# A four-layer mixture-of-experts block: rope's turning in four transfers, the gather a step ahead, combine first, exp behind the copies

## The reference

```python
# x: 16 sequences of 256 rows and 128 columns
h = layernorm(x) * (1 + ca) + sa
x = x + ga * wavelet_attention(h)           # the prologue
h = layernorm(x) * (1 + cb) + sb
for l in range(4):                          # the loop of this study
    h = rms(x, ln1_w[l])
    q, k, v = h @ wq[l], h @ wk[l], h @ wv[l]     # 16 query heads, 4 key heads of 64
    q, k = q * cos + rot_half(q) * sin, k * cos + rot_half(k) * sin
    a = softmax(q k^T / 8 + causal) v
    x = clip(x + a @ wo[l], -100, 100)
    h = rms(x, ln2_w[l])
    # 8 experts of width 256, the two best of each row, weighted by their softmax
    x = clip(x + sum_e comb_e * (silu(h @ wg[l, e]) * (h @ wu[l, e])) @ wd[l, e], -100, 100)
x = x1 + gb * x
```

## Time and profile before

| | |
|---|---|
| median of 3 runs | 3637.83 us (3637.82 to 3639.13) |
| profiled execution | 3605.28 us, span 3603.5 us |
| mean granted clock of PE | 0.891 |
| busy share PE, DVE, ACT, Pool | 75%, 63%, 56%, 52% |

### The profile page before, as it was taken

How to read it: one execution, slowest core, us unless ns; L and a number is a source line. 1 busy time by engine, 2 the same in 40 slices (tenths; PEclk the granted TensorE clock), 3 DMA queues, 4 the chain that set the end, 5 groups by cost and what they waited for, 6 DMA issues and landing times.

```text
span 3603.5 us, 67188 instructions
## 1 busy us (share of the span) xinstructions
PE 2710.9 (75%) x20406; PEld 2157.3 (60%) x20406; DVE 2263.4 (63%) x8164; ACT 2015.8 (56%) x7080; POOL 1860.3 (52%) x1662
## 2 busy tenths in 40 slices
PE   5227777788778887888778876888778877887573
PEld 2225555666657665676567765676566665676462
DVE  5775555666666666666666665675666766666343
ACT  3126556566656656666556665665666665666321
POOL 0025555545565556555665556545665565555413
PEclk9558888999999999999989998999999998999765
DMA  9112222555236642555255633654256622553374
GB/s 377 70 49 62 62 64 62 163 179 172 69 116 200 214 126 85 165 179 155 65 162 183 211 100 95 190 166 137 67 180 208 195 84 90 178 180 111 124 253 132
DMA packets 327990, 511.67 MB, mean 142 GB/s; under 512 B 56353, under 2 KB 175681, under 8 KB 327105
## 3 DMA queue, kind: packets, MB, share of 16 engines
q1 hardware_dynamic: 311248, 473.79, 42.5%
q0 software_dynamic: 16384, 33.59, 3.0%
HBM read 316.58 MB, written 106.69 MB: 117 GB/s over the span
## 4 chain that ended last, share of the span: by engine, by line
PE 37%; ACT 16%; DVE 15%; POOL 14%; SPq 7%; DMA 6%; issue 5%; POOLq 0%; DVEq 0%
ACT arena L1049 9%; PE psum L778 6%; SPq L626 5%; PE psum L796 5%; POOL rows_in L1274 5%; POOL arena L1283 4%; DVE arena L1546 3%; DMA arena<-arena 3%; PE psum L846 2%; PE psum L753 2%; DVE arena L1568 2%; PE psum L798 2%; PE psum L896 2%; DMA arena<-rows_out,arena 2%; POOL arena L1300 2%
## 5 line engine op out<-in xcount | busy, mean ns | idle before, releaser
L1049 ACT ACTIVATE arena<-arena 128x128 f32<-128x128 f32 (+1 forms) x2048 | 900.9, 446 | 46.8 <-DVE arena L1572 46.8
L1283 POOL TENSOR_TENSOR arena<-arena 128x512 f32<-128x512 f32 (+1 forms) x512 | 743.9, 1476 | 251.4 <-DVE arena L1577 249.2
L778 PE MATMUL psum<-arena 128*128 128x128 f32 x3072 | 509.8, 308 | 384.3 <-ACT arena L1056 192.4
L1300 POOL TENSOR_TENSOR arena<-arena 128x512 f32<-128x512 f32 x320 | 409.5, 1280 | 573.5 <-DMA arena<-arena 573.2
L778 PEld LDWEIGHTS psum<-arena 128*128 128x128 f32 x3072 | 368.1, 154 | 506.0 <-ACT arena L1056 258.0
L1056 ACT COPY arena<-psum 128x384 f32<-128x384 f32 x1024 | 450.9, 480 | 284.0 <-PE psum L778 283.0
L1581 DVE COPY arena<-psum 128x512 f32<-128x512 f32 x256 | 176.4, 689 | 553.9 <-PE psum L798 553.9
L753 PE MATMUL psum<-arena 64*128 64x128 f32 (+1 forms) x4096 | 445.3, 358 | 10.9 <-DVE arena L1568 6.0
L1568 DVE CUSTOM_DVE_ANT_0 arena<-psum,arena 128x256 f32<-128x256 f32 x1024 | 429.6, 420 | 0.0
L1546 DVE TENSOR_TENSOR arena<-psum,arena 128x512 f32<-128x512 f32 x640 | 390.5, 675 | 7.4 <-POOL arena L1300 4.1
L1049 ACT ACTIVATION_READ_ACCUMULATOR arena<-arena 128x1 f32 x2048 | 389.7, 190 | 0.0
(11 more groups left out here) (199 smaller groups left out, 5608.4 us busy)
## 6 DMA issues: line engine op xcount, KB each, us to landing
gu<-gu_kept SPq DMA_DIRECT2D x320, 512.0 KB, 4.4
arena<-arena SPq DMA_DIRECT2D x1280, 64.0 KB, 2.0
wd<-wd_kept SPq DMA_DIRECT2D x320, 256.0 KB, 4.1
arena<-rows_in SPq DMA_DIRECT2D x320, 64.0 KB
rows_out<-arena SPq DMA_DIRECT2D x320, 64.0 KB, 2.6
rows_in<-arena SPq DMA_DIRECT2D x34, 512.0 KB, 7.5
rows_out<-arena SPq DMA_DIRECT2D x34, 512.0 KB, 7.0
gu_kept<-w_hi SPq DMA_DIRECT2D x32, 256.0 KB
```

Of the source, the lines that this page charges most:

```text
L778: mm = T.transpose(psum[:, t_bank(key), j * P:(j + 1) * P], probs[:, q, i, j * P:(j + 1) * P], ident)
L1049: ins = A.activation(a, a, ACT.Exp, bias=negmax[:, q, k:k + 1], accum_out=rowsum[:, q, k:k + 1])
L1283: ins = G.tensor_tensor(a, a, r[:, :, t:t + 1].broadcast_to([P, 4, P * (t + 1)]), ALU.mult)
L1300: G.tensor_tensor(QKT[it % 2][:, 2 * u:2 * u + 2, :].rearrange("p a b -> p (a b)"), own_part[:, k, :], turned_part[:, k, :], ALU.add).then ...
```

## The change

- Rope: the columns of wq and wk and the tables are reordered so that the two halves of a head lie on alternate partitions (`halves_in_turn`). A swap of neighbours then takes two transfers for a group of units: 3 units, then 2, so four a step for twenty. `to_turn` and `turned_part` hold all five units; the cosine product goes straight to QKT, and Pool adds in place after one wait a group.
- Pool: root stands ahead of normalise(0) and of the gather, scatter(it - 2) stands behind root (it was scatter(it - 1) at the step's end), and the gather is for it + 2, behind normalise(0), or behind normalise(2) at the end of a batch.
- DVE: combine stands ahead of place 0.
- ACT: square_rows and scale_rows come earlier; exp(0) stands behind copies(2), exp(1) behind copies(3) and ahead of the copy of v; exp(2) and exp(3) are cut in two around the first part of places 5 and 7; copy_y comes after the second part.
- One half-step of each batch is moved from place 7 of step 6 to place 6 of step 5.

```diff
+def halves_in_turn(w):
+    lead = w.shape[:-1]
+    return np.swapaxes(w.reshape(*lead, w.shape[-1] // HD, 2, HD // 2), -2, -1).reshape(w.shape)
...
-                          (5, (0, 1, 2, 3, 4, 5, 7)), (6, (0, 1, 2, 3, 4, 5, 7))):
+                          (5, range(8)), (6, range(6))):
...
 # turn_halves, SP
-                for u in units:
-                    n = 5 * it + u
-                    k = n % ROPE_RING
-                    s_was_read(sp, ("qk", it, u))
-                    for r in range(4):
-                        here, there = r * 32, (r ^ 1) * 32
-                        sp.dma_start(turned_part[there:there + 32, k, :], to_turn[here:here + 32, k, :]) \
-                            .then_inc(sem(f"turned_in{k}"), 16)
+                s_was_read(sp, ("qk", it, units[-1]))
+                us = slice(units[0], units[-1] + 1)
+                for r in range(2):
+                    sp.dma_start(turned_part[1 - r:P:2, us, :], to_turn[r:P:2, us, :]) \
+                        .then_inc(sem(f"turned_in{units[0]}"), 16)
...
 # ACT, the loop
+            def moe_end(b, hs):
+                if hs % 2 == 1 and hs > 1:
+                    copy_y(b * PT + hs // 2 - 1)
...
                 place(it, 0)
+                place_end(it, 0)
                 if old:
                     copy_probs(it - 1, 2)
-                place(it, 1)
-                if now:
-                    exps(it, 0)
-                if old:
-                    copy_probs(it - 1, 3)
-                if now:
-                    copy_v(it)
-                place(it, 2)
-                if now:
-                    exps(it, 1)
                 if coming:
                     square_rows(it + 1)
-                place(it, 3)
+                if now:
+                    exps(it, 0)
+                place(it, 1)
+                place_end(it, 1)
+                if old:
+                    copy_probs(it - 1, 3)
+                if now:
+                    exps(it, 1)
+                    copy_v(it)
                 if coming:
                     scale_rows(it + 1)
+                place(it, 2)
+                place_end(it, 2)
+                place(it, 3)
+                place_end(it, 3)
...
+                if now:
+                    exps(it, 2, range(2))
                 place(it, 5)
                 if now:
-                    exps(it, 2)
+                    exps(it, 2, range(2, 4))
+                place_end(it, 5)
...
 # Pool, the loop
-                if coming and it + 1 >= B:
-                    gather(it + 1)
-                if now:
-                    normalise(it, 0)
                 if coming:
                     root(it + 1)
+                if it >= 2:
+                    scatter(it - 2)
+                if now:
+                    normalise(it, 0)
+                if B <= it + 2 < NIT and (it + 2) % HB != 0:
+                    gather(it + 2)
...
                 if now:
                     normalise(it, 2)
+                if B <= it + 2 < NIT and (it + 2) % HB == 0:
+                    gather(it + 2)
                 if coming:
                     rope_adds(it + 1, range(N_QK1, N_QK))
-                if old:
-                    scatter(it - 1)
...
 # DVE, the loop
                 if old:
                     invert(it - 1, 3)
+                if coming and it + 1 >= B:
+                    combine(it + 1)
                 place(it, 0)
...
-                if coming and it + 1 >= B:
-                    combine(it + 1)
                 if old:
                     update_x(it - 1)
```

More of the change, by code:

```diff
@@ L342, in bass_program @@
         tiles = arena.take(2).bitcast(U32)
-        ROPE_RING = 3
         dead_at_end = arena.at
-        own_part = arena.take(ROPE_RING, 512)
-        to_turn = arena.take(ROPE_RING, 512)
-        turned_part = arena.take(ROPE_RING, 512)
+        to_turn = arena.take(N_QK, 512)
+        turned_part = arena.take(N_QK, 512)
         QKT = [arena.take(2 + NH // 2, S) for _ in range(2)]
@@ L384, in bass_program @@
         back_last = arena.take(LAST_RING, ST, 2, C)
[L385 removed]
+        assert arena.at <= dead_at_end + 2 * N_QK * 512 + 2 * (2 + NH // 2) * S
         ZERO_ROWS = 8
@@ L453, in gate_side, with keys_and_queries @@
             return U_AT["gate", g, j] % U_RING
+        def keys_and_queries(it, u):
+            return QKT[it % 2][:, 2 * u:2 * u + 2, :].rearrange("p a b -> p (a b)")
         def kv_head(q, half):
@@ L618, in turn_halves @@
             def turn_halves(it, units):
-                for u in units:
-                    n = 5 * it + u
-                    k = n % ROPE_RING
-                    s_was_read(sp, ("qk", it, u))
-                    for r in range(4):
-                        here, there = r * 32, (r ^ 1) * 32
-                        sp.dma_start(turned_part[there:there + 32, k, :], to_turn[here:here + 32, k, :]) \
-                            .then_inc(sem(f"turned_in{k}"), 16)
+                s_was_read(sp, ("qk", it, units[-1]))
[3 more added lines that the diff above has]
+                        .then_inc(sem(f"turned_in{units[0]}"), 16)
             phase_done(sp, 0)
-            turn_halves(0, range(N_QK))
+            turn_halves(0, range(N_QK1))
+            turn_halves(0, range(N_QK1, N_QK))
             for it in range(NIT):
@@ L1042, in _, with exps @@
             A.copy(wqk_hi, wqk).then_inc(sem("wqk_hi_ready"), 1)
-            def exps(it, q):
+            def exps(it, q, heads=range(4)):
                 act.wait_ge(sem("negmax_ready"), 4 * it + q + 1)
-                for k in range(8):
+                for k in range(2 * heads[0], 2 * heads[-1] + 2):
                     i, t = k // 2, k % 2
@@ L1049, in exps @@
                     ins = A.activation(a, a, ACT.Exp, bias=negmax[:, q, k:k + 1], accum_out=rowsum[:, q, k:k + 1])
-                ins.then_inc(sem("exp_done"), 1)
+                if heads[-1] == 3:
+                    ins.then_inc(sem("exp_done"), 1)
             def copy_probs(it, q):
@@ L1159, in place, with place_end @@
                     moe(*half_steps[it, p])
+            def place_end(it, p):
+                if (it, p) in half_steps:
+                    moe_end(*half_steps[it, p])
             for it in range(-1, NIT + 1):
@@ L1191, in _ @@
                 place(it, 4)
+                place_end(it, 4)
                 if now:
@@ L1205, in _ @@
                     copy_ranks(it - 1)
+                if now:
+                    exps(it, 3, range(2))
                 place(it, 7)
                 if now:
-                    exps(it, 3)
+                    exps(it, 3, range(2, 4))
+                place_end(it, 7)
             for hs in range(HS):
                 moe(NB - 1, hs)
+                moe_end(NB - 1, hs)
         @block.gpsimd
@@ L1294, in rope_adds @@
             def rope_adds(it, units):
+                pool.wait_ge(sem(f"turned_in{units[0]}"), 32 * (it + 1))
                 for u in units:
[L1297 to L1301, removed]
+                    G.tensor_tensor(keys_and_queries(it, u), keys_and_queries(it, u), turned_part[:, u, :], ALU.add) \
+                        .then_inc(sem("rope_done"), 1)
             for it in range(-1, NIT + 1):
@@ L1306, in _ @@
                     normalise(it - 1, 3)
-                if coming and it + 1 >= B:
-                    gather(it + 1)
+                if coming:
+                    root(it + 1)
+                if it >= 2:
+                    scatter(it - 2)
                 if now:
                     normalise(it, 0)
-                if coming:
-                    root(it + 1)
+                if B <= it + 2 < NIT and (it + 2) % HB != 0:
+                    gather(it + 2)
                 if old:
@@ L1321, in _ @@
                     normalise(it, 2)
+                if B <= it + 2 < NIT and (it + 2) % HB == 0:
+                    gather(it + 2)
                 if coming:
                     rope_adds(it + 1, range(N_QK1, N_QK))
-                if old:
-                    scatter(it - 1)
+            scatter(NIT - 1)
             for s in range(B):
@@ L1775 @@
     given["ln2_T"] = np.asarray(inputs["L0_ffn_ln2_w"]).T
-    wq, wk = (head_blocks(np.asarray(inputs[n])) for n in ("L0_ffn_wq", "L0_ffn_wk"))
+    wq, wk = (halves_in_turn(head_blocks(np.asarray(inputs[n]))) for n in ("L0_ffn_wq", "L0_ffn_wk"))
     wo = np.asarray(inputs["L0_ffn_wo"])
```

20 lines of the change are left out of this document (9 added, 11 removed).

## The result

The changed kernel takes 3500.78 us (median of 4, 3495.73 to 3505.69) against 3637.85: ratio 0.9625, 95% interval 0.9612 to 0.9638. Forecast were 3482 us and 3325 to 3590. The profiled executions differ by less: the span is 3493.9 us after and 3603.5 before, 109.6 us, where the medians differ by 137. The profiled execution of the kernel before was 32.6 us shorter than its median, the one of the changed kernel 5.1. So my step by which the ratio 1.009 of median to profiled execution would hold for the new kernel didn't hold (here it is 3500.78/3495.73 = 1.001). The traces can be held against the sum only at 109.6, and there it was 154.

A forecast was written before the change was run, and what follows sets the result against it. No engine is full, so waits between engines bound the kernel. Savings of 61 + 50 + 9 + 15 + 14 + 5 = 154 us take 3605.3 to 3451, times 1.009: 3482 us, range 3325 to 3590.

The forecast's parts named there:

- Steps without a gather: Attention-only steps: normalise wait 4.7, transposes 1.0 and h's scaling 3.0 gained, copy_h's delay 1.1 lost; 7.6 us, 8 steps: 61.
- Attention-only with a gather: ACT replaces Pool in the 5.65 us wait; the 3.02 us at h go, less 0.2: 2.8 us, 18 steps: 50.
- adds in a row on Pool at no cost in MoE steps: Turning transfers: issues fall from 20 to 4 a step, adds follow back to back; second group ends 2.4 us earlier.
- bound of 7.3 us: Upper bound on x_ready after invert, combine held by two late adds as well; 4.7 us forecast, 1.7 if never held.
- rival D: Combine on DVE is held longer by Pool; each us past 4.7 costs 48; at 10 us, 3738 us; chance 0.08.
- scatter behind root: Pool's four scatters leave the path from last add to normalise(3), 4.9 us; behind root they were taken as covered.
- literal reading: DVE could slip in after Pool's first, shorter instruction: some 1.9 us less in 48 steps, about 90 us lower.
- Halving exp, with copy_y: ACT in MoE steps: split exp(2), exp(3) gain 1.0 us, late tanh costs 0.8; later copy_y costs 0, up to 0.5.
- The factor 1.009: Ratio of median 3637.8 to profiled 3605.3 us before, applied to the forecast 3451 to give 3482 us.
- B: Combine on DVE isn't held by Pool; exp(0) starts 3 us earlier, together 147 us more, 3334 us; chance 0.20.
- C: The turning's transfers land late; at 8 us they cost 78 and some 20 in MoE steps: 3581 us; chance 0.15.
- E: Nothing gained: MoE steps lose what others win, exp(1) ahead of place 2, copy_y behind exp; 3638 us; chance 0.05.

The follow-up runs named there:

- normalise behind combine: Changed kernel with one wait added on Pool: normalise(old 3) first waits for x_ready, so combine runs without Pool beside it; 3429.61 us, ratio 0.9424.
- choose first: Changed kernel with Pool waiting for choose of the old sequence before its three rope adds in a row; 3466.62 us, ratio 0.9539.
- choose free: Changed kernel with both Pool waits, for choose before the first rope adds and for x_ready before normalise(old 3); 3384.39 us, ratio 0.9313.

## Why the prediction was right, and where it wasn't

**Right: the direction, the waits that go, and that combine is held.** The wait at the turning of h went. In the steps without a gather it was 24.1 us, 3.0 a step, as in the sum. In the attention-only steps with one, ACT took Pool's place. PE's wait for low_rows came as forecast, and so did ACT's for x_ready: 199.7 us in 48 steps, 4.2 each, about 4 forecast. The experiment with normalise behind combine shows that the hold causes them.

**Steps without a gather: 70.9 us against 61, but not by the terms.** PE stood 37.5 us less in the 8 steps (92.8 to 55.3), where the sum had 4.7 + 3.0 - 1.1 = 6.6 a step, 53. The wait for normalise gave 3.2 a step (38.9 to 13.5 us), not the whole 4.7. The delay of copy_h took 1.5 (11.3 to 23.2 us in front of the projections), not 1.1. The other 33.4 us are PE's busy time, for which the sum had 8, as 1.0 back at the transposes. One instruction took 132 ns before and 115 after (268.49/2040 and 235.12/2043), a ratio of 0.87, that of the granted clocks 0.86/0.98 = 0.88. Counted from these shares, PE ran at the lower of its two levels (1.2 GHz) for some 100 us of the stretch before and 12 after. I had no term for the clock; that it rose because PE waits less is my reading and no run shows it by itself. So the agreement is in part luck: a term too large and one that was missing.

**Attention-only with a gather: 50.8 against 50.** The wait changed its owner as forecast. But PE's busy time in these 18 steps fell as well, from 605.3 to 578.1 us, at a mean clock of 0.91 before and 0.89 after. Why, isn't shown, and the total doesn't prove the terms.

**The step that failed: adds in a row on Pool at no cost in MoE steps.** The landing was as sized or shorter. But alone the new turning cost 0.5% and saved nothing, and in the changed kernel the old one is 0.5% faster. The bound of 7.3 us and rival D have late adds holding combine. Nothing in the prediction has the first group of adds meeting choose, and in MoE steps they have no term. The first MoE steps of a batch pay, +35.5 us where I had -2: choose first gives 20 of them back, the old turning 21. In the 8 steps without a gather the transfers are worth 1.1 us, not 2.4. There the sum didn't even need them: of the 7.3 us by which normalise was to be earlier, 4.9 were the scatter's, and PE's wait was 4.7.

**The step that was too simple: scatter behind root.** 4.9 us a step was right where there is no combine (5.0 measured). With combine, the four scatters had also kept normalise from starting beside it: with them back at the end the MoE steps are 2.2 us shorter, the first ones of a batch 6.1.

**Combine's hold.** x_ready comes 3.8 us after invert in 36 of 48 steps, 4.7 forecast. I had DVE stand still between the two pairs of products for the whole of normalise, 2.9 us. In the trace one product waits for the first instruction of normalise, gets in, and the next one waits for the second. So the literal reading, by which DVE slips in after Pool's first instruction, is what most products did. It was worth 0.9 us, not the 1.9 that I gave it, since the next product is held again.

**Mis-sized terms.** Halving exp, with copy_y: 21 to 27 us by the run, against 0.2 us a step net. MoE without a gather: 5.5, not 15 (and four times 4 are 16); with the old turning it would have been 14.7. Batch ends 12 against 14. The unheld combine: 71 us, or 82 with choose free, not 147. The factor 1.009 has nothing behind it: the sum came out 44 us too large, the factor gave 31 of them back, and so the forecast lies only 19 us from the median. That is luck.

**Rivals.** B didn't happen: the median product took 0.74 us. C didn't: 3.0 us to land, 5.0 at most. D didn't: in the six combines at 8.3 us DVE first waited for rows, 28.1 us in all. E was there in part, by another path: the 24 MoE steps with a gather lost 40 us in all, through the two holds (choose first gives 20 us of the first steps' 35.5 back, normalise behind combine 34) and not, as far as these runs show, through exp(1) or copy_y. Still open: why freeing combine alone gives nothing in the other 18 MoE steps with a gather (+4 us), where freeing choose alone gives 12 and both 24. The place of exp(1), ahead of place 2, wasn't tried by itself.

## What to carry to other kernels

Before two engines' work is brought to start at the same signal, ask which of the two holds the other: here a DVE product that met an elementwise instruction of Pool's ended only behind it, so four products that need 1.4 us alone took some 3.5 as a rule and 4.5 in the step shown. Grouping transfers also groups the work behind them: beside single adds choose took 2.1 us, beside three in a row 3.4 to 4.5. When an instruction leaves a path, look at whom its slowness had been letting pass. And when a total agrees with a forecast, part it into waits and busy time before believing the terms.

## What the runs showed of the hardware

- A DVE product of two SBUF tensors that met an elementwise Pool instruction mostly took 1.1 to 1.9 us where it takes 0.35 alone, and ended 0.15 us behind it. Of the 96 products over 0.6 us after the change, 92 waited for one Pool instruction, two for two and two for three, although the Pool instructions followed without a gap. The small tensor_scalar of line 1572 (8 columns) is different: of 47 long ones before, 18 ended behind two Pool instructions, one of them after 2.99 us. The Trainium skill (SBUF — State Buffer, Who interferes with whom) has the contention, and that the first to issue keeps the shared ports for its whole instruction (said there of DVE's modes with two ports). How many Pool instructions in a row a waiting DVE instruction lets pass is what these rows add, and what decides it isn't shown.
- DVE instructions that read PSUM kept their time beside the same kind of Pool work: of those of L1566 and L1568 before that started inside an elementwise Pool instruction, 313 and 328, none took over 0.293 and 0.422 us, as without company (0.295 and 0.422). The reciprocal of line 1577, on SBUF alone, wasn't held either: 57 of them took at most 0.204 us.
- Pool's issue of scatters and gathers held DVE little: of the 22 instructions of line 1572 before that started beside one and met no elementwise work, the median took 0.17 us, as without company, and the longest 0.39. Combine's four products took 1.22 us beside it in the run with the scatter at the step's end.
- Swapping neighbouring partitions by transfers of every second one, 256 and 384 KB, landed in 3.0 us (2.5 to 5.0), less than the 4.4 us of 512 KB from DRAM.
